# Expert stage of a graph layer and mixture-of-experts kernel: the second layer runs one unit further behind the first, the turn back two units further, with rings of four

## What is computed

```python
x = x + relu(adj @ (item_feat @ W_item.T + b_item) + layernorm(x) @ W_user.T + b_user)   # 10000 x 10000 adjacency
h = layernorm(x)                                    # 10000 tokens of 128
probs = softmax(h @ gate_w + gate_b)                # 8 experts, the best one is taken
pos = place of the token in its expert; kept = pos < 1563
hmid = relu(buf @ w1[e] + b1[e])                    # 128 -> 512
y = (hmid @ w2[e] + b2[e]) * (prob * kept)          # 512 -> 128
x = x + nan_to_num(y)
```

## Time and profile before

| | |
|---|---|
| median of 3 runs | 1433.86 us (1433.54 to 1437.7) |
| the profiled execution | 1426.02 us, of it the span 1423.8 |
| TensorE, products | busy 1359.3 us (95%) |
| VectorE | busy 1171.0 us (82%) |
| ScalarE | busy 979.0 us (69%) |
| GpSimd | busy 544.1 us (38%) |
| DMA queues | 435.88 MB, 306 GB/s in the mean |

### The profile page before, as it was taken

The page is one execution under the profiler, slowest core; times in us unless marked ns, Lnnn a source line. Parts: engine busy times, 40 slices in busy tenths (PEclk is TensorE's granted clock), DMA queues, the critical chain, the costliest instruction groups (busy, mean ns, idle before and its releaser), DMA issues. The chain is left out here.

```text
span 1423.8 us, 20288 instructions
## 1 busy us (share of the span) xinstructions
PE 1359.3 (95%) x6278; PEld 1106.8 (78%) x6278; DVE 1171.0 (82%) x1725; ACT 979.0 (69%) x1010; POOL 544.1 (38%) x359
## 2 busy tenths in 40 slices
PE   7999999999999999999999999999999997788895
PEld 6888888888888888888888888888888785566663
DVE  7998988989889888898898988988989875567665
ACT  5777866767768767676677676766776766566662
POOL 0001235053152350531523505325135365555656
PEclk9999999999999999999999999999999998999988
DMA  9999999999999999999999999999999961222210
GB/s 339 356 392 407 402 381 351 367 348 372 368 357 357 367 357 364 354 367 362 355 360 360 358 372 357 364 361 358 354 372 349 350 225 48 76 71 75 62 47 3
DMA packets 89259, 435.88 MB, mean 306 GB/s; under 512 B 22289, under 2 KB 24992, under 8 KB 89217
## 3 DMA queue, kind: packets, MB, share of 16 engines
q1 hardware_dynamic: 68505, 417.98, 79.5%
q0 software_dynamic: 17632, 12.24, 3.1%
q10 hardware_dynamic: 3080, 5.12, 1.1%
HBM read 422.80 MB, written 23.50 MB: 313 GB/s over the span
## 5 line engine op out<-in xcount | busy, mean ns | idle before, releaser
L676 DVE TENSOR_TENSOR a_lo<-raw,a_hi 128x2000 fp32r<-128x2000 f32 (+1 forms) x400 | 862.3, 2187 | 125.0 <-ACT a_hi L476 122.4
L476 ACT CAST a_hi<-raw 128x2000 fp32r<-128x2000 f32 (+1 forms) x400 | 721.0, 1825 | 184.4 <-PE bank L1083 112.1
L1081 PE MATMUL bank<-a_hi,h_hi 128*128 128x500 f32 x1560 | 625.5, 401 | 1.5 <-ACT a_hi L476 0.8
L1083 PE MATMUL bank<-a_hi,h_lo 128*128 128x500 f32 x1560 | 605.9, 388 | 0.0
L1092 PE MATMUL bank<-a_lo,h_hi 128*128 128x500 f32 x1560 | 417.8, 388 | 0.0
L1081 PEld LDWEIGHTS bank<-a_hi,h_hi 128*128 128x128 f32 x1560 | 293.3, 188 | 66.4 <-issue 11.4
L1083 PEld LDWEIGHTS bank<-a_hi,h_lo 128*128 128x128 f32 x1560 | 294.0, 188 | 58.5 <-issue 4.4
L1092 PEld LDWEIGHTS bank<-a_lo,h_hi 128*128 128x128 f32 x1560 | 293.2, 188 | 59.0
L977 POOL TENSOR_TENSOR late<-ve,neghalf 125x4 f32<-125x4 f32 x20 | 57.2, 2860 | 635.6 <-DVE ve L693 635.6
L985 POOL DMA_INDIRECT records<-late,slot x80 | 175.0, 2187 | 23.3 <-issue 23.3
L1049 POOL DMA_INDIRECT out<-raw x128 | 130.4, 1019 | 91.4 <-DVE raw L940 46.8
(11 more groups left out here) (124 smaller groups left out, 942.3 us busy)
## 6 DMA issues: line engine op xcount, KB each, us to landing
raw<-adj_m SPq DMA_DIRECT2D x380, 1000.0 KB, 6.2
raw<-adj_m SPq DMA_DIRECT2D x20, 500.0 KB
raw<-records SPq DMA_DIRECT2D x32, 202.1 KB
late<-items_t SPq DMA_DIRECT2D x19, 256.0 KB, 4.7
xb<-x ACTq DMA_DIRECT2D x20, 224.0 KB
raw<-w SPq DMA_DIRECT2D x8, 258.5 KB
raw<-w SPq DMA_DIRECT2D x8, 256.0 KB
out<-raw POOLq DMA_INDIRECT x128
```

What stands on the lines that cost most here:

```text
L476: last = nc.scalar.copy(a_hi[:, g % HI_RING, 0:m], raw[:, g % RAW, 0:m])
L676: last = v.tensor_tensor(a_lo[:, g % RAW, 0:m], raw[:, g % RAW, 0:m], a_hi[:, g % HI_RING, 0:m].bitcast(F32), ALU.subtract)
L1081: nc.tensor.matmul(acc[q][:, 0:BLOCK], h_hi[:, k * HID:(k + 1) * HID], a, start=(k == 0), stop=False)
L1083: last = nc.tensor.matmul(acc[q][:, 0:BLOCK], h_lo[:, k * HID:(k + 1) * HID], a, start=False, stop=False)
```

## The change

The lags become LAG_Y = 4 and LAG_OUT = 6. hm and yT become rings of four, which yout already is. VectorE copies the four token numbers of each slot into a ring of their own, tokq, just ahead of the sum, and the scatters take them from there; so SyncE's load_rec no longer waits for the scatters to land. The weights get a semaphore for each layer. w1 of an expert is loaded ahead of the records of its first unit and waits for the split of the expert two before it; w2 is loaded behind those records and waits, as before, for the last take_y of that expert. take_mid waits for w2, whose load also carries the biases. steps() writes out 14 steps instead of 6 ahead of its loop, and the drain has six steps.

```diff
-LAG_IN, LAG_MID, LAG_Y, LAG_OUT = 1, 2, 3, 4
-YRING = 4
+LAG_IN, LAG_MID, LAG_Y, LAG_OUT = 1, 2, 4, 6
+YRING = HM_RING = YT_RING = 4
...
-        hm = tail(128, 2, FC, UNIT)
+        hm = tail(128, HM_RING, FC, UNIT)
-        yT = tail(128, 2, UNIT)
+        yT = tail(128, YT_RING, UNIT)
+        tokq = tail(SLOT_P, YRING, 4)
...
-            for k in range(EARLY, BODY):
-                step(0, k, k)
-            with eng.Fori(1, UNITS // BODY) as i:
+            for s in range(EARLY, 2 * BODY):
+                step(s // BODY, s % BODY, s)
+            with eng.Fori(2, UNITS // BODY) as i:
...
-            def load_weights(r):
+            def load_w1(r):
                 w1_e = w1[bass.ds(expert[r], 1), :, :].rearrange("o p n -> (o p) n")
+                if r >= 2:
+                    sp.wait_ge(w1_lo_ready, r - 1)
+                sp.dma_start(wb1[:, r % 2, :], w1_e).then_inc(w1_loaded[r % 2], 16)
+
+            def load_w2(r):
                 w2_e = w2[bass.ds(expert[r], 1), :, :].rearrange("o p n -> (o p) n")
                 if r >= 2:
                     sp.wait_ge(yT_ready, (r - 1) * UNITS_E)
-                sp.dma_start(wb1[:, r % 2, :], w1_e).then_inc(weights_loaded[r % 2], 16)
-                sp.dma_start(wb2[:, r % 2, :], w2_e).then_inc(weights_loaded[r % 2], 16)
+                sp.dma_start(wb2[:, r % 2, :], w2_e).then_inc(w2_loaded[r % 2], 16)
...
                 if n >= BODY:
                     sp.wait_ge(yout_ready, n - BODY + 1)
-                    sp.wait_ge(sent[n % YRING], (n - BODY) // YRING * 64 + 64)
...
-                if n >= BODY and n % UNITS_E == 2:
-                    load_weights(n // UNITS_E)
+                if n >= BODY and n % UNITS_E == 0:
+                    load_w1(n // UNITS_E)
                 load_rec(n)
+                if n >= BODY and n % UNITS_E == 0:
+                    load_w2(n // UNITS_E)
...
             def take_mid(i, k):
                 n = i * BODY + k
-                if not isinstance(i, int) or n >= 2:
-                    act.wait_ge(y_done, n - 1)
+                act.wait_ge(w2_loaded[k // UNITS_E % 2], (i + k // BODY + 1) * 16)
+                if not isinstance(i, int) or n >= HM_RING:
+                    act.wait_ge(y_done, n - HM_RING + 1)
...
             def take_y(i, k):
                 n = i * BODY + k
                 act.wait_ge(y_done, n + 1)
-                if not isinstance(i, int) or n >= 2:
-                    act.wait_ge(y_turned, n - 1)
+                if not isinstance(i, int) or n >= YT_RING:
+                    act.wait_ge(y_turned, n - YT_RING + 1)
...
                     dve.wait_ge(sent[u], (i * (BODY // YRING) + k // YRING) * 64)
+                v.tensor_scalar(tokq[:, u, :].unsqueeze(2).bitcast(U32), recq[:, r, :, C_TOK:C_TOK + 1].bitcast(U32),
+                                0, None, ALU.add)
                 v.tensor_tensor(yout[:, u, :, :], yf.rearrange("p (j d) -> p j d", j=4), recq[:, r, :, 0:HID],
                                 ALU.add).then_inc(yout_ready, 1)
...
-                        ap=recq[:, n % BODY, j, C_TOK:C_TOK + 1].bitcast(U32), axis=0),
+                        ap=tokq[:, n % YRING, j:j + 1].bitcast(U32), axis=0),
```

More of the change, by code:

```diff
@@ L253, in build @@
         x1_chain_done = sem("x1_chain_done")
-        weights_loaded = [sem(f"weights_loaded{i}") for i in range(2)]
+        w1_loaded = [sem(f"w1_loaded{i}") for i in range(2)]
+        w2_loaded = [sem(f"w2_loaded{i}") for i in range(2)]
         recq_loaded = [sem(f"recq_loaded{i}") for i in range(BODY)]
@@ L429, in _ @@
             sp.wait_ge(lo_used, (BLOCKS - 1) * GROUPS + RAW + weight_slots)
-            load_weights(0)
+            load_w1(0)
+            load_w2(0)
             sp.wait_ge(lo_used, (BLOCKS - 1) * GROUPS + RAW + early_slots)
@@ L433, in _ @@
                 if n == EARLY:
-                    load_weights(1)
+                    load_w1(1)
+                    load_w2(1)
                 if n == 4:
                     store_last_x1()
-                if n >= BODY and n % UNITS_E == 2:
-                    load_weights(n // UNITS_E)
+                if n >= BODY and n % UNITS_E == 0:
+                    load_w1(n // UNITS_E)
                 load_rec(n)
+                if n >= BODY and n % UNITS_E == 0:
+                    load_w2(n // UNITS_E)
             sp.wait_ge(passed_on[0], BLOCKS // 2 * TILES * 16)
@@ L567, in split_w1 @@
                 e = i * 2 + k // UNITS_E
-                act.wait_ge(weights_loaded[k // UNITS_E], (i + 1) * 32)
+                act.wait_ge(w1_loaded[k // UNITS_E], (i + 1) * 16)
                 if not isinstance(i, int):
@@ L592, in take_mid @@
                 n = i * BODY + k
-                if not isinstance(i, int) or n >= 2:
-                    act.wait_ge(y_done, n - 1)
+                act.wait_ge(w2_loaded[k // UNITS_E % 2], (i + k // BODY + 1) * 16)
+                if not isinstance(i, int) or n >= HM_RING:
+                    act.wait_ge(y_done, n - HM_RING + 1)
                 for f in range(FC):
                     act.wait_ge(mid_done, n * FC + f + 1)
-                    nc.scalar.activation(hm[:, k % 2, f, :], ps_mid[f][:, 0:UNIT], ACT.Relu,
+                    nc.scalar.activation(hm[:, k % HM_RING, f, :], ps_mid[f][:, 0:UNIT], ACT.Relu,
                                          bias=bias_of(k, f)).then_inc(hm_ready, 1)
@@ L602, in take_y @@
                 act.wait_ge(y_done, n + 1)
-                if not isinstance(i, int) or n >= 2:
-                    act.wait_ge(y_turned, n - 1)
-                nc.scalar.activation(yT[:, k % 2, :], ps_y[:, 0:UNIT], ACT.Identity,
+                if not isinstance(i, int) or n >= YT_RING:
+                    act.wait_ge(y_turned, n - YT_RING + 1)
+                nc.scalar.activation(yT[:, k % YT_RING, :], ps_y[:, 0:UNIT], ACT.Identity,
                                      bias=bias_of(k, FC)).then_inc(yT_ready, 1)
@@ L1223, in second @@
                 for f in chunks:
-                    last = nc.tensor.matmul(ps_y[:, 0:UNIT], wb2[:, w, f * HID:(f + 1) * HID], hm[:, k % 2, f, :],
+                    last = nc.tensor.matmul(ps_y[:, 0:UNIT], wb2[:, w, f * HID:(f + 1) * HID], hm[:, k % HM_RING, f, :],
                                             start=(f == 0), stop=(f == FC - 1))
@@ L1235, in turn_y @@
                     last = nc.tensor.transpose(ps_out[0:SLOT_P, j * HID:(j + 1) * HID],
-                                               yT[:, k % 2, j * SLOT_P:(j + 1) * SLOT_P], ident)
+                                               yT[:, k % YT_RING, j * SLOT_P:(j + 1) * SLOT_P], ident)
                 last.then_inc(y_turned, 1)
```

## The result

The changed kernel took 1428.28 us (median of 10, 1419.98 to 1433.08) against 1434.53 us (10 runs, 1432.44 to 1437.7): ratio 0.9946, interval 0.9924 to 0.9969. I had forecast 1443 us, slower; the time lies in the range, but the sign was wrong. Three more comparisons, on three different chips, gave 0.9996 (0.9970 to 1.0023), 0.9970 (0.9947 to 0.9993) and 1.0014 (0.9988 to 1.0039). Their mean is 0.998, some 3 us faster, which so few of them can't tell from no change. None shows the +9 us of the forecast (1.006).

A forecast was written before the change was run, and what follows sets the result against it. It took the expert stage's loop to be set by GpSimd's scatters and VectorE, with TensorE's signals late. Drain +10.4, turn_y -2.6 and token ring +1.3 gave +9.1 on 1433.86: 1443 us, range 1427 to 1450 (own mechanism 1438 to 1453).

The forecast's parts named there:

- The bound: Expert stage: GpSimd's scatters and VectorE's chain set the loop; TensorE's signals arrive late, when scatters end; 13.86 us per two units.
- Rings and LAG_Y: Second layer one unit later, hm and yT in rings of four: nothing waits for the room; 0 us.
- turn_y out of the stall: TensorE's turn_y runs inside the stall while second() waits, saving its own issue: -2.6 us, between 0 and -5.3.
- The drain: Behind the last unit, two more units pass through GpSimd at 5.2 us each: +10.4 us, between 10.1 and 11.1.
- the stalls shift with it and keep their number: Start of the stage: scatters begin two steps later, but this hides none of the longer drain.
- at an unchanged pace step 33 turns unit 27: End of the loop: step 33 turns unit 27 and not 29, leaving GpSimd two units more behind it.
- R1: Rival: the loop shortens as GpSimd's pause shrinks 1.26 us in each of 12 pairs, -15.1; 1428 us, chance 0.24.
- The token ring: VectorE's token copy ahead of L940 delays GpSimd 0.1 us per round, 13 times: +1.3 us, between 0 and 2.9.
- SyncE: Record loads no longer wait 49.0 us for scatters: worth 0, as L579 never idles; upper end 5.4 us slower.

The follow-up runs named there:

- (3, 5): Changed kernel with LAG_Y 3 and LAG_OUT 5 instead of 4 and 6; 1430.77 us, ratio 0.9978 to the kernel before.
- (4, 5): Changed kernel with LAG_Y 4 and LAG_OUT 5 instead of 4 and 6; 1432.88 us, ratio 0.9975 to the kernel before.
- a_none: Changed kernel with no scatter in the expert stage and no wait for one, kept output rows left out; 1383.45 us, ratio 0.9653 to the kernel before.
- b_none: Kernel before with no scatter in the expert stage and no wait for one, kept output rows left out; 1378.71 us, ratio 0.9617.
- b_again: Kernel before, unchanged, run for a second trace; loop 204.4 us, drain 31.5 us.
- b_rows32: Kernel before with all four scatters per unit, each of 32 rows instead of 98, on the faster chip; 1400.45 us, ratio 1.0018.
- b_one: Kernel before with one scatter per unit instead of four, three quarters of the rows left out; 1385.0 us, ratio 0.9653.
- b_two: Kernel before with two scatters per unit instead of four, half of the rows left out, on the faster chip; 1387.2 us, ratio 0.9920.
- (5, 6): Changed kernel with LAG_Y 5 and LAG_OUT 6 instead of 4 and 6; 1437.02 us, ratio 1.0006; on the faster chip 1398.33 us, 1.0012.
- a_sent_wait: Changed kernel with SyncE's wait for the scatters of unit n-8 put back ahead of each record load; 1430.77 us, ratio 0.9992.

## Why the prediction was wrong

*The bound.* Right, and the experiments made it firm: TensorE's signals are late while GpSimd issues scatters, and the loop falls from 202 to 160 us without them. The wait at L1235 was the end of that and not its cause. The writing of the rows, which I suspected next, is not it either: dropped rows do the same.

*Rings and LAG_Y: 0.* Nothing speaks against it as a sum; (3, 5) and (4, 5) are within 2.1 us of each other, in loops and medians. But LAG_Y moves one second layer out of the loop (20.3 and 18.0 us between units 2 and 6) and into the drain (32.9 and 36.5).

*turn_y out of the stall: -2.6, between 0 and -5.3.* The rounds from unit 10 on are no shorter: 148.3 and 149.2 us. About 0, within a spread of some 10 us.

*The drain: +10.4.* It was the right mechanism and a size somewhat too small: 29.6 us in the mean of the three traces with lags 3 and 4, 42.1 in the four of the change, +12.5. In the trace after, late signals reach into the drain: behind the one of 9.8 us GpSimd stands still for 7.77 us, where I had it at work without pause. The span ends 42.4 us behind step 33's turn back and not 35.

*The step that failed* is the sentence "the stalls shift with it and keep their number", and with it "at an unchanged pace step 33 turns unit 27". The loop went from 204.4 to 190.1 us in the mean, -14.4, where I had -1.3. Two things are in it.

From unit 2 to 6 it is 3.2 us: one second layer and two turn backs no longer fall into the loop but into the drain, where the scatters cover them. A turn back takes 0.44 us, a second layer 2.64, from its start at 1383.59 to the next step's transposes in the trace before:

```profile
1386.23 0.50 PE L1200 MATMUL bank<-cst,raw 98*128 98x98 f32 x4
```

My sum left this out. a_none against b_none shows it alone, -2.9.

From unit 6 to 10 it is 12.1 us, and without scatters 0 (22.3 us in b_none and in a_none): it hangs on the late signals. The first scatter of a unit and the first long waits for a signal, before:

```profile
1204.56 1.07 POOL L1049 DMA_INDIRECT out<-raw  x1 [4.51 <-DVE raw L940]
1221.99 0.69 DVE L923 TENSOR_TENSOR raw<-bank,raw 98x512 f32<-98x512 f32 x1 [8.34 <-remote]
```

and after:

```profile
1211.36 0.96 POOL L1061 DMA_INDIRECT out<-raw  x1 [10.10 <-DVE raw L952]
1237.32 0.69 DVE L933 TENSOR_TENSOR raw<-bank,raw 98x512 f32<-98x512 f32 x1 [4.02 <-remote]
1241.60 0.59 ACT L615 ACTIVATE raw<-bank,raw 128x392 f32<-128x392 f32 x1 [5.12 <-remote]
```

The scatters begin about 7 us later, but the first long wait ends 15 us later. The only earlier one after is short (1.95 us at L933, ending 1219.23), and until unit 10 TensorE goes at its full rate. The stalls therefore don't shift with the units; two or so of them leave the loop. -14.4 + 12.5 is what remains, with 1 us of later start in these traces: no change that one comparison tells safely.

*R1* came near the size of the gain in the loop (-17.7) by another way: it had every round shorter, and none got shorter. That its 1428 us is the time measured first is luck. *The token ring: +1.3.* 0.08 us an instruction, within the bounds. *SyncE: 0.* Right for the records, 0.3 us at L588. The weights were missing from the sum. In the trace before nothing waited for them; in b_again the split did for 5.5 us, in b_rows32 for 17.4, in b_one and b_two for 0.6 at most. The change takes this wait away, for a few us where it occurs.

*A second fault* is one of reading: the terms came from one trace, an execution 8 us under its own median, and the forecast had no row from which its spread, as large as each term, could be seen.

Open: why the first signal that is late by over 3 us arrives 17 us after the first scatter in each of the three traces with lags 3 and 4, and 26 to 30 us after it in the four of the change. (5, 6) against (4, 6) points to a part for turn_y's freedom, and a_sent_wait (27.7 us between units 6 and 10 with lags 4 and 6) to one for the loads, from one trace each. Whether number or rows of the scatters count was tried only where signals were in time.

## What to carry to other kernels

A lag moves work and transfers out of the loop and into the drain. Count both, the work of each engine too; where one serial engine (here GpSimd, 5.2 us a unit) closes the chain, later is only useful for the units that then pass before that engine disturbs the others. When idle time hangs on a signal that comes late, ask what was going on when it came, and take that away in an experiment before any order of stages is tuned: here one scatter per unit instead of four (in a kernel that leaves out the other rows) was worth 49 us, the lags 3 us in the mean. And repeat a trace before its stretches are subtracted.

## What the runs showed of the hardware

TensorE's semaphore signals reached ScalarE and VectorE 2 to 10 us after the recorded end of the instruction (a median of 4.0 us in the trace before, and 9.8 at most, in the drain of the trace after) while GpSimd issued indirect transfers back to back, even with nearly all rows dropped by the bound. With one such transfer per unit or none they reached ScalarE's take_y within 0.1 us. The same kernel took 1397 us on one chip and 1432 to 1434 on four others. The traces of its variants put the difference into this stage: unit 2 starts at 1195 to 1200 us on all chips, and the loops are 160 to 166 us on the one and 184 to 207 with four scatters on the others (180 with the rows dropped). The Trainium skill's "Perfetto Trace Analysis", section "Per-instruction lifecycle: what the profiler-reported window actually captures", separates a matmul's estimated end from its signal; the runs agree that they can be far apart, and show that the gap was not work of TensorE: with the same products on TensorE it was gone once the scatters of another engine were.
